# Reordering the prologue of a fused attention and mixture-of-experts kernel: splits, first tanh and second maximum moved

## The reference, cut to what matters

```python
xn = layer_norm(x, ln_g, ln_b)
cn = layer_norm(context, cln_g, cln_b)
q = (xn @ Wq).reshape(b, n, HEADS, DIM_HEAD).transpose(0, 2, 1, 3) * scale
kv = cn @ Wkv
k, v = (kv[..., :DIM_HEAD], kv[..., DIM_HEAD:])
sim = jnp.einsum('bhid,bjd->bhij', q, k)
attn = jax.nn.softmax(sim, axis=-1)
out = jnp.einsum('bhij,bjd->bhid', attn, v)
out = out.transpose(0, 2, 1, 3).reshape(b, n, INNER) @ Wo
ff = xn @ Wff1
h, gate = (ff[..., :FF_INNER], ff[..., FF_INNER:])
out = out + jax.nn.silu(gate) * h @ Wff2
...
x = x + jnp.tanh(g_xattn[0]) * _L0_xattn_ref(_layernorm(x), ctx_1024, ...)
x = x + jnp.tanh(g_ffn[0]) * _L0_ffn_ref(_layernorm(x), ...)
```

## Time and profile before

| | |
|---|---|
| median of 3 runs | 534.79 us (534.63 to 535.72) |
| profiled execution | 536.77 us, of which the span from first to last instruction is 534.6 |
| TensorE matmul busy | 496.8 us, 93% of the span |
| DVE, ACT, POOL busy | 406.7, 327.2, 288.4 us |
| granted TensorE clock, mean | 0.982 |

### The profile page before, as it was taken

The page is one execution under the profiler, slowest core; times in us unless marked ns, Lnnn a source line. Parts: engine busy times, 40 slices in busy tenths (PEclk is TensorE's granted clock), DMA queues, the critical chain, the costliest instruction groups (busy, mean ns, idle before and its releaser), DMA issues.

```text
span 534.6 us, 13846 instructions
## 1 busy us (share of the span) xinstructions
PE 496.8 (93%) x4026; PEld 482.5 (90%) x4026; DVE 406.7 (76%) x1253; ACT 327.2 (61%) x1092; POOL 288.4 (54%) x332
## 2 busy tenths in 40 slices
PE   7779999999999999999999999999999989999940
PEld 7669999999999999999999999999998779999930
DVE  6677778788787878786888888787677888888830
ACT  2576657675665675657566756675567727767730
POOL 2488627553643554364445436553685334677773
PEclk9899999999999999999999999999999999999995
DMA  5552300102003010301210030004398976788753
GB/s 170 196 155 85 99 2 33 31 25 105 31 20 118 21 29 11 118 32 30 78 61 21 20 118 31 10 28 141 118 345 298 408 267 141 132 136 145 114 65 39
DMA packets 40213, 53.85 MB, mean 101 GB/s; under 512 B 4598, under 2 KB 34219, under 8 KB 39147
## 3 DMA queue, kind: packets, MB, share of 16 engines
q1 hardware_dynamic: 31856, 41.48, 23.6%
q0 software_dynamic: 8000, 11.86, 11.9%
q10 hardware_dynamic: 314, 0.01, 0.0%
HBM read 28.15 MB, written 25.21 MB: 100 GB/s over the span
## 4 chain that ended last, share of the span: by engine, by line
PE 60%; DVE 11%; issue 8%; DMA 7%; POOLq 5%; ACT 5%; POOL 3%; SPq 0%; DVEq 0%; ACTq 0%
PE bank L1544 12%; PE bank L1546 11%; PE bank L1545 11%; DMA out_x<-norm_probs,th 5%; PE bank L1625 5%; POOLq L729 4%; PE bank L1637 4%; PE bank L1730 4%; PE bank L1720 4%; PE bank L1641 3%; PE bank L1628 2%; PE bank L1735 2%; PE bank L1559 2%; DVE norm_probs L1012 2%; ACT norm_probs L818 2%
## 5 line engine op out<-in xcount | busy, mean ns | idle before, releaser
L628 POOL TENSOR_TENSOR norm_probs<-norm_probs,rden 128x512 f32<-128x512 f32 x64 | 66.5, 1040 | 101.2 <-DVE rden L1192 100.4
L1544 PE MATMUL bank<-acts,weights 128*128 128x256 f32 x384 | 110.1, 287 | 5.3 <-POOL weights L599 5.3
L1545 PE MATMUL bank<-acts,weights 128*128 128x256 f32 x384 | 108.6, 283 | 0.0
L1546 PE MATMUL bank<-acts,weights 128*128 128x256 f32 x384 | 108.3, 282 | 0.0
L818 ACT ACTIVATE norm_probs<-bank,nmax 128x128 f32<-128x128 f32 x256 | 90.4, 368 | 23.8 <-DVE nmax L1148 23.8
L633 POOL TENSOR_TENSOR acts<-uf,acts 128x256 fp32r<-128x256 f32 x64 | 47.5, 742 | 68.7 <-ACT acts L806 68.7
L1544 PEld LDWEIGHTS bank<-acts,weights 128*128 128x128 f32 x384 | 73.3, 191 | 6.2 <-issue 5.0
L742 POOL DMA_INDIRECT out_x<-norm_probs,th x39 | 60.7, 1557 | 25.6 <-DMA out_x<-norm_probs,th 14.2
L1546 PEld LDWEIGHTS bank<-acts,weights 128*128 128x128 f32 x384 | 73.1, 190 | 0.0
L1545 PEld LDWEIGHTS bank<-acts,weights 128*128 128x128 f32 x384 | 73.0, 190 | 0.0
L806 ACT ACTIVATE acts<-uf 128x256 fp32r<-128x256 f32 x64 | 26.8, 419 | 61.3 <-DVE uf L1217 61.2
(11 more groups left out here) (251 smaller groups left out, 1544.5 us busy)
## 6 DMA issues: line engine op xcount, KB each, us to landing
parked<-stage SPq DMA_DIRECT2D x12, 512.0 KB, 3.5
weights<-parked SPq DMA_DIRECT2D x6, 1024.0 KB
slot_rows<-tf SPq DMA_DIRECT2D x8, 680.0 KB, 6.6
spare<-slot_rows SPq DMA_DIRECT2D x39, 136.0 KB
ct<-in_ctx SPq DMA_DIRECT2D x8, 256.0 KB, 2.7
xs<-in_x SPq DMA_DIRECT2D x8, 256.0 KB, 4.8
stage<-in_L_ffn_up_w SPq DMA_DIRECT2D x8, 256.0 KB, 2.8
stage<-in_L_ffn_down_w SPq DMA_DIRECT2D x8, 256.0 KB, 3.1
```

Source lines behind the costliest of these rows:

```text
L628: pool.tensor_tensor(pr[:, s % 2], pr[:, s % 2], rden[:, s % 2, :].unsqueeze(2).broadcast_to((P, 4, P)), ALU.mult).then_inc(probs_ready, 1)
L1544: pe.matmul(ps, wts[1], mov[0], start=first, stop=False, skip_group_check=True)
L1545: pe.matmul(ps, wts[0], mov[0], start=False, stop=False, skip_group_check=True)
L1546: return pe.matmul(ps, wts[0], mov[1], start=False, stop=last, skip_group_check=True)
```

## The change

Ahead of the first iteration: the queries of the first two pairs wait for half of the low parts of wq0 and wq1 only (columns 0 to 511), DVE makes wq0's in two halves, the second behind the values. Wkv's high part goes from DVE to ACT, behind chunk 3, and its low part behind the context's transposes. The split of the gate weights goes from there into step 3. SP issues chunk 6 ahead of the second group's context and x, and chunk 5 behind them.

In the first iteration: the tanh, u and uf of unit 0 stand ahead of its exponentials on ACT and ahead of the reciprocal on DVE. The low parts of chunks 6 and 5 go from POOL to DVE (steps 0 and 1). DVE's second maximum stands ahead of the layer-norm statistics of group 1. POOL splits chunks 7, 8, 10, 9 in steps 2, 3, 4, 5. ACT's high part of a chunk stands behind the copy of the transposed probabilities, not ahead of it. Chunk 4 is announced to TensorE in four parts.

```diff
-EARLY = 6
-CHUNK_SLOT = {0: [6], 1: [7], 2: [8], 3: [9], 4: [10]}
-LO_ON_POOL = (2, 4, 5, 6, 7, 8, 9, 10)
+CHUNK_SLOT = {2: 7, 3: 8, 4: 10, 5: 9}
+LO_ON_POOL = (2, 4, 7, 8, 10, 9)
+HI_ORDER = (1, 2, 3, 4, 6, 5, 7, 8, 10, 9)
+LO_PARTS = {1: 2, 2: 2, 4: 4}
...
-            for n in range(NCA):
+            for n in range(5):
                 load_chunk(n)
-                if n == EARLY - 1:
-                    load_ctx(1)
-                    load_x(1)
+            load_chunk(6)
+            load_ctx(1)
+            load_x(1)
+            load_chunk(5)
+            for n in range(7, NCA):
+                load_chunk(n)
...
                     done = pool.tensor_tensor(lo_i, src_i, hi_i.bitcast(F32), ALU.subtract)
-                done.then_inc(chunk_split_done[n], 1)
+                    if (i + 1) % (4 // LO_PARTS.get(n, 1)) == 0:
+                        done.then_inc(chunk_split_done[n], 1)
...
             split_lo(4)
-            split_lo(5)
             iteration(0, first=True)
...
                 for s in range(NU + 2):
                     u = g * NU + s
-                    if 1 <= s <= NU:
-
-                        act.wait_ge(mix_freed, mix_index(f"FF{s - 1}", g, first, last) + 1)
-                        if not (first and s < 3):
-                            act.wait_ge(ff2_done, u - 2)
-                        act.activation(uT[0][:, (s - 1) % 2, :], uf[:, :], ACT.Copy).then_inc(uh_done, 1)
+                    if 1 <= s <= NU and not (first and s == 1):
+                        hidden_high(s - 1, g, first, last)
+                    if first and s == 0:
+                        hidden_tanh(s, g, first, last)
...
-                    if first:
-                        for n in CHUNK_SLOT.get(s, []):
-                            split_hi(n)
+                    if first and s == 0:
+                        hidden_high(s, g, first, last)
...
                         probs_hi(u - 1, first and s == 1)
...
+                    if first and s == 1:
+                        split_hi(5)
+                    if first and s in CHUNK_SLOT:
+                        split_hi(CHUNK_SLOT[s])
+                    if s < NU and not (first and s == 0):
+                        hidden_tanh(s, g, first, last)
...
             split_hi(3)
+            landed(act, 0)
+            act.activation(wkv[0][:, :, :], stage[:, 0, 0:KT * P].rearrange("p (k n) -> p k n", k=KT), ACT.Copy
+                           ).then_inc(kv_hi_done, 1)
             transposed_hi("TXc", None, False, False, cnT[0])
...
             split_hi(4)
-            split_hi(5)
+            split_hi(6)
             iteration(0, first=True)
...
             transposed("TXx", None, False, False, 0)
-            early_lo(1)
+            early_lo(1, 0)
             first_lo(xnT, 1, xnT_ready)
             transposed("TXc", None, False, False, 0)
...
+            key_weights()
+            first_lo(cnT, 2, cnT_ready)
             dve.wait_ge(down_rows_in, 32)
             dve.tensor_tensor(down_rows, down_rows, shared_rows, ALU.add).then_inc(down_sums_done, 1)
-            first_lo(cnT, 2, cnT_ready)
...
             values_lo(None, False, False, 0)
+            early_lo(1, 1)
...
+                    if first and s == 0:
+                        hidden_values(s)
...
+                    if s == 1 and first:
+                        dve.wait_ge(ctx_loaded, 32)
+                        dve.wait_ge(x_in[1], 16)
+                        small_steps(2)
...
                         dve.reciprocal(rden[:, s % 2, :], den[:, s % 2, :]).then_inc(rden_done, 1)
+                    if first and s < 2:
+                        early_lo((6, 5)[s])
+                    if first and s == 3:
+                        gate_parts()
...
+                if first and pair == 2:
+                    split(pe, 1)
+                    split(pe, 2)
...
-                        chunk([4, 8][(s - 1) // 4])
+                        chunk([4, 8][(s - 1) // 4], s if s < 5 else None)
...
-            split(pe, 1)
-            split(pe, 2)
+            split(pe, 1, 1)
+            split(pe, 2, 1)
             queries(0, None, False, False, 0)
```

More of the change, by code:

```diff
@@ L448, in landed, with split @@
             eng.wait_ge(stage_full[buffer(n)[1]], stage_value(n))
[L450 to L452 removed]
+        def split(eng, n, part=None):
+            if n >= NCA:
+                eng.wait_ge(ring_ready, n - NCA + 1)
+            else:
+                eng.wait_ge(chunk_split_done[n], LO_PARTS.get(n, 1) if part is None else part)
         def turned_values(b):
@@ L796, in probs_hi, with hidden_high, hidden_tanh @@
                 act.activation(pT[0][:, :], t_ps[:, :], ACT.Copy).then_inc(pTh_done, 1)
+            def hidden_high(s, g, first, last):
+                u = g * NU + s
+                act.wait_ge(mix_freed, mix_index(f"FF{s}", g, first, last) + 1)
+                if not (first and s < 2):
+                    act.wait_ge(ff2_done, u - 1)
+                act.activation(uT[0][:, s % 2, :], uf[:, :], ACT.Copy).then_inc(uh_done, 1)
+            def hidden_tanh(s, g, first, last):
+                u = g * NU + s
+                b = mix_ps[mix_bank(f"FF{s}", g, first, last)]
+                act.wait_ge(mix_filled, mix_index(f"FF{s}", g, first, last) + 1)
+                if not (first and s == 0):
+                    act.wait_ge(u1_done, u)
+                act.activation(th[:, :], b[:, GT:2 * GT], ACT.Tanh, scale=0.5).then_inc(tanh_done, 1)
             def iteration(g, first=False, last=False):
@@ L827, in iteration @@
                         probs_hi(u - 1, first and s == 1)
-                    if s < NU:
-                        b = mix_ps[mix_bank(f"FF{s}", g, first, last)]
-                        act.wait_ge(mix_filled, mix_index(f"FF{s}", g, first, last) + 1)
-                        if not (first and s == 0):
-                            act.wait_ge(u1_done, u)
-                        act.activation(th[:, :], b[:, GT:2 * GT], ACT.Tanh, scale=0.5).then_inc(tanh_done, 1)
+                    if first and s == 1:
+                        split_hi(5)
+                    if first and s in CHUNK_SLOT:
+                        split_hi(CHUNK_SLOT[s])
+                    if s < NU and not (first and s == 0):
+                        hidden_tanh(s, g, first, last)
                     if s in PARK_STEPS and not first and not last:
@@ L1139, in small_steps, with hidden_values @@
                     at_step += 1
+                def hidden_values(s):
+                    u = g * NU + s
+                    b = mix_ps[mix_bank(f"FF{s}", g, first, last)]
+                    dve.wait_ge(tanh_done, u + 1)
+                    dve.scalar_tensor_tensor(u1[:, :], th[:, :], 1.0, b[:, GT:2 * GT], ALU.add, ALU.mult
+                                             ).then_inc(u1_done, 1)
+                    if s in (1, 2, 3):
+                        small_steps(1)
+                    if s == 6 and not first:
+                        hot_choices(g - 1)
+                    dve.wait_ge(u1_done, u + 1)
+                    if not (first and s == 0):
+                        dve.wait_ge(u_ready, u)
+                    dve.scalar_tensor_tensor(uf[:, :], b[:, 0:GT], 0.5, u1[:, :], ALU.mult, ALU.mult
+                                             ).then_inc(mix_freed, 1)
                 for s in range(NU + 2):
@@ L1645, in iteration, with chunk @@
             def iteration(g, first=False, last=False):
-                def chunk(n):
+                def chunk(n, part=None):
                     if first:
-                        split(pe, n)
+                        split(pe, n, part)
                 def scores(s):
```

55 lines of the change are left out of this document (19 added, 36 removed).

## The result

| | before | after |
|---|---|---|
| median, 20 runs each | 535.70 us (534.02 to 537.70) | 533.76 us (531.42 to 536.34) |
| ratio | 1 | 0.9964 (0.9948 to 0.9979) |
| profiled execution, span | 536.77, 534.6 | 534.93, 532.9 |
| TensorE, DVE, ACT, POOL busy | 496.8, 406.7, 327.2, 288.4 | 496.9, 406.6, 327.5, 284.1 |

The change makes the kernel 1.9 us faster (1.1 to 2.8). The direction was forecast, the size was not: 3.3 was forecast. The 533.76 lies 0.2 above the predicted range; of its distance to 531.5, 2.3, 0.9 is the baseline, whose median over 20 runs is that much above the median of three with which the sum began.

A forecast was written before the change was run, and what follows sets the result against it. TensorE was taken as the bound, busy without a break from 62.00 us, its earlier stillnesses as time to save. The parts bring the mark 3.3 earlier; the median 534.79 less 3.3 gives 531.5, range 529.8 to 533.6.

The forecast's parts named there:

- the mark: Start of the scores of step 7, behind which nothing waits: forecast at 58.7 against 62.00.
- part 3: Step 0: chunk 6 lands at 22, exponentials at 23.8, POOL's normalisation waits 1.1, transposes at 27.7 against 31.58.
- Part 1: Start of the queries: two low-part instructions on POOL suffice instead of four, start at 15.5, 1.9 earlier.
- Part 2: Clock at the queries' start: stays at 2.4 GHz; DVE's three instructions begin at 18.1, 20.6 against 23.46, 2.9 earlier.
- Rival A: The clock falls nonetheless at the queries, delaying what follows by 0.8: gain 2.5, 532.3; chance 0.10.
- Rival C: Chunk 6 lands at 24.5, tanh and exponentials queue behind its high part on ACT: gain 1.5, 533.3; chance 0.11.
- Part 4: Step 1: exponentials at 27.3 against 32.64, probabilities' low part at 32.05 against 35.61; TensorE waits 2.0.
- part 5: Steps 2 to 5: a circle over DVE and ACT, period 5.08; uf of unit 5 at 53.4, 3.85 earlier.
- Part 6: Projection of step 6: TensorE waits 1.6 for POOL's low part of chunk 9; scores of step 7 at 58.7.
- Rival B: Chunk 9 is done in time, no stall at the projection of step 6: gain 4.9, 529.9; chance 0.12.
- Rival E: Slower: POOL held up 0.98 for each split of chunks 7, 8, 10, 9: 535.4; chance 0.04.
- rival D: The gain reaches 62 us and is lost in the last stage, with its DMA loads: 534.8; chance 0.05.

The follow-up runs named there:

- e11: The kernel before once more, no edit, for a second profile: 536.52 us, ratio 1.0009.
- e1: The kernel after once more, no edit: 533.74 us, ratio 0.9973 against the kernel before.
- e2: The kernel after with 14 and 16 idle transposes filling TensorE's two pauses: 535.98 us, ratio 1.0006 against the kernel before.
- e3: The kernel after with the gate weights' split moved from step 3 to the end of step 8: 533.28 us, ratio 0.9957 against the kernel before.
- e4: The kernel after with POOL's splits a step earlier, chunks 7, 8, 9, 10 in steps 1 to 4: 533.18 us, ratio 0.9959.
- e6: The kernel after with DVE's low part of chunk 5 moved from step 1 to step 2, behind the maximum: 530.48 us, ratio 0.9934.
- e8: The kernel after with the edits of e3 and e6 together: 529.54 us, ratio 0.9880 against the kernel before.
- e9: e8 with chunk 9 announced to TensorE in two halves: 529.02 us, ratio 0.9874 against the kernel before.
- e12: e9 with 8 idle transposes ahead of the first probabilities' transposes: 529.21 us, ratio 0.9884 against the kernel before.
- e10: The kernel before with only the halves of Wq, plus 36 idle transposes ahead of the first probabilities' transposes: 539.11 us, ratio 1.0071.

## Why the forecast was right in its direction and wrong in its size

The times of the forecast are set 1.0 earlier here, for the landing. That is the most that can be taken out: by e11 some 0.65 of it arrives at the mark, and then all that is called late below is 0.35 less late from part 3 on.

- **Part 1** was right: queries at 14.5, seen at 14.44; so was the price of half the low parts, 1.97 from POOL's start at 12.47 to the queries for 1.98.
- **Part 2** was right for the place that it looked at: 1.00 at 14 to 20 us, the first hidden product at 19.6, seen at 19.42. Rival A (the clock falls behind that pause) did not happen.
- **Part 3** had the mechanism and the end right, the load of chunk 6 not: it left at 15.94, and ACT, which waited 1.29 for it, began at 21.86 for the 21.0 taken (22 less 1.0), just outside the cover to 21.7. The exponentials came at 23.08 for 22.8. Then the normalisation was held up, 1.93 for 1.04 (1.1 extra forecast, 0.9 seen), with the transposes at 26.7, seen at 26.86. Rival C, that load at 24.5 (23.5), is out.
- **Part 4** was right to 0.3: the wait for DVE was foreseen as 2.0 and was 1.85, with chunk 5's subtraction stretched to 1.82 beside POOL's normalisation. The Trainium skill ("SBUF — State Buffer", Who interferes with whom) has the two exclude each other, whoever issues first; both rows agree, POOL losing the first time and DVE the second.
- **What failed first** is the step from parts 3 and 4 to part 5. The first pause (1.6 forecast) was compared by its length with the 2.20 that had cost nothing, the second (2.0 forecast) with nothing, and the circle was then started at full clock. The clock fell behind the second: 1.51 and 1.85 with 3.3 us of work between. It cost 1.4 here, and 1.5 by e1 against e2. Of the four profiles with both pauses left in (after, e1, e3, e4) three lost the clock; of those with the second one filled or removed (e2, e6, e8, e9, e12) none did. But length and number do not tell when: the pairs of the kernel before (2.20 and 1.44, 2.1 of work between) and of e11 (2.36 and 1.45) are longer in sum and closer together, and neither lost it. Whether the second pause needs the first was not run either: no kernel has the second alone. The Trainium skill ("TensorE: Matmul & The Clock Gate", A second HAM failure mode: psum-queue depth-cycling) tells of short stillnesses between groups of matmuls that are frequent enough to make the clock swing; after, e1 and e3 fit that, before, e11 and e4 had such stillnesses and kept 1.00.
- **What failed second** is the gate weights in part 5, costed at nothing, at 0.4 uncovered. ACT's copy was no cover: the two instructions stand on the circle, and POOL's chunk 7 and normalisation held them up to 0.70 and 0.97. e3 measures 1.06 (6.47 to 5.41). The other 0.3 of that step is left in e3; there DVE's low part of queries (39.14, 0.68 in the kernel after) stands between uf and the maximum, which the forecast's period does not hold. No run took it out.
- The rest of **part 5** held: without these two the steps are 5.0 to 5.1 (e6), 5.41 with chunk 7.
- **Part 6** had the mechanism and its place; the stall was 0.95 for 1.6, mostly because the last step of uf was 4.76 for 5.08, and because TensorE's way to it took 3.5 for 3.3. Rival B, no stall, is out; e9 shows that its removal is worth 1.3 at the mark.
- Rival E is out: the splits of chunks 7, 8, 10 and 9 took 2.82, 2.83, 3.00 and 2.81.
- **The sum.** Forecast for the mark 58.7 less 1.0, 57.7; seen 60.40, 2.7 later (2.4 with 0.65 for the landing). The chain of uf explains it: 0.2 at unit 1, then 1.4, 1.4, 0 and less 0.3. Behind the mark nothing was lost (472.6 and 472.5), so there is no sign of rival D in this kernel, within the 1 us or so by which such stretches differ between profiles of one kernel (472.6 and 473.9 before). The forecast called TensorE busy without a break from the mark on; the kernel before has waits of 0.82 and 0.57 at 437 us. e2 shows a loss of the kind that D described, at that place, without a known cause.
- **Mark and time.** At equal landing the mark is 0.8 to 1.3 earlier, the time 1.9 (1.1 to 2.8) and 1.5 (0.7 to 2.1) less. These agree within their noise; the 3.3 forecast is outside all of them.

Three things stay open: what decides that the clock falls, with the kernel before, e11 and e4 keeping it through two pauses; whether the second pause would do it alone; and why e2 has its longer wait for the rows at 434 us.

## What to carry to other kernels

A pause that cost nothing in one kernel is no licence for a shorter one in another: here pauses of 1.1 to 1.9 us lost TensorE's clock three times in four, where 2.20 and 1.44 had not. Where a forecast leaves pauses, price the slow clock (1.5 here) as a case of its own, and read the granted clock behind each pause; removing the pause (e6) gave time, filling it (e2, e10, e12) did not. An instruction moved "beside other work" is free only if its own engine's circle has room there, whatever its size; ask also which engine works on SBUF at that moment. And test an edit alone before crediting it: the earliest gain here, the halves of Wq, made the kernel slower without its companions, by the rows because it kept a buffer from the next load.
